# A mixture-of-experts decoder layer: TensorE's expert numbers read one a tile instead of sixteen at once

## The chip, the cores and the metric

The kernel runs on one core of a Trainium2 chip. The metric is the device time in microseconds (us) of one execution, the median of three. Besides the runs that only give a time there is one profiled execution, and every row below comes from it.

## The reference

One decoder layer on `x` of shape (8, 256, 256), with a context of (8, 120, 256). It has three parts, each followed by a layer norm: causal self-attention with 16 heads, a slot-attention block with a GRU cell in three iterations, and a feed-forward part with a shared MLP and 8 experts of which each token takes 2. The change touches the experts alone:

```python
router_probs = softmax(x @ gate_w + gate_b)
expert_values, expert_indices = top_k(router_probs, k=2)
expert_values = expert_values / (expert_values.sum(-1) + 1e-09)
h = gelu(einsum('bsd,edi->bsei', x, ew1) + eb1)        # D = 256, I = 1024, E = 8
all_outputs = einsum('bsei,eid->bsed', h, ew2) + eb2
moe_out = einsum('bse,bsed->bsd', weights_E, all_outputs)
return x + mlp(x, sh_w1, sh_b1, sh_w2, sh_b2) + moe_out
```

## The kernel before

All matmuls of the experts are done on two float16 halves of each number. The 2 x 2048 choices of the router are sorted by expert into tiles of 128 rows, each tile of one expert. There are `NTILE` = 39 tiles. Which expert a tile belongs to is known only at run time: VectorE writes the 39 numbers as integers into `tile_e`, one row of the on-chip memory, while the shared MLP still runs (line 2147).

The instructions of each engine are written out by hand and each engine takes its own in order, with semaphores between them. An engine that needs the expert of a tile reads it from `tile_e` into registers (`experts_from`, a TENSOR_LOAD), and every address of a weight is worked out from such a register. TensorE's program in the expert stage is a loop over `i`. In each round it turns the gathered rows of tile `i + 3` (`turn`, two transposes, line 1872), and then runs `tile_pair(i + 2, ..., i, ...)`: the first layer ("up") of tile `i + 2` mixed with the second layer ("down") of tile `i`. One `tile_pair` has eight chunks `k`. A chunk has six up matmuls of 128 columns (line 2254), one down matmul of 512 columns (line 2262) and one of 256 (line 2263). So a full round has 48 + 8 + 8 + 2 = 66 matmuls. The order of TensorE's program shows what stands between the matmuls for the addresses: in each chunk four instructions of line 2254 (the order calls them ISA, the trace FUSED_REGOPS) and one of line 2262 (REGISTER_ALU, in the trace ALU_OP). They compute with registers.

The expert numbers reach TensorE's registers in three reads, of at most `LOADED` = 16 numbers each. The first is in the shared MLP, two matmul groups before the first transposes (`first_experts`). The second stands in front of `tile_pair(16, ...)`, behind the transposes of tile 17. The third, of the last 7 numbers, stands in front of `tile_pair(32, ...)`:

```python
if (i + 2) % LOADED == 0:
    expert += experts_from(mybir.EngineType.PE, i + 2)
tile_pair(i + 2, expert[i + 2], i, expert[i])
```

VectorE (`experts_vector`) reads the same numbers for its own use in three such reads of its own. ScalarE does the gelu, VectorE the biases and the low halves, GpSimd gathers rows of later tiles and adds finished rows into memory by indirect DMA.
Of the kernel before, what the change touches and what calls it, by code (L numbers as in the profile page):

```python
# [34 lines left out]
def decoder_layer(nc, a, out):  # L35
# [5 lines left out]
    E, _, I = a["L0_ffn_ew1"].shape  # L41
# [11 lines left out]
    NTILE = 2 * T // P + E - 1  # L53
# [3 lines left out]
    with top:  # L57
        def sb(ctx, name, shape, dt=F32):
            return ctx.enter_context(nc.sbuf_tensor(name, shape, dt))
# [47 lines left out]
        tile_e = sb(top, "tile_e", [P, NTILE], I32)  # L107
# [368 lines left out]
        with ExitStack() as c:  # L476
# [90 lines left out]
            for j in range(LOW_FROM, ITEMS):  # L567
                for place, n in enumerate(room(j)):
                    n = min(n, LOW_SHARES * PIECES - made)
# [1109 lines left out]
        with ExitStack() as c:  # L1679
# [172 lines left out]
            LOADED = 16  # L1852
            first_experts = []

            def experts_from(engine, i):

                _, values = nc.values_load_multi_w_load_instructions(
                    tile_e[0:1, i:min(i + LOADED, NTILE)], engines=(engine,), min_val=0, max_val=E - 1,
                    skip_runtime_bounds_check_because="a count of at least zero, cut at E - 1 where it is made",
                    bass_reorder=False)  # L1860
                return list(values)

            def turn(i):

                PE.wait_ge(rows_in[i % 2], 16 * (i // 2 + 1))
                if i == 0:
                    PE.wait_ge(count_mm, 2)
                if i >= 1:
                    PE.wait_ge(g_lo, i)
                    PE.wait_ge(g_hi, i)  # L1870
                for ch in range(DC):
                    mm = PE.transpose(ps[:, 7, ch * P:ch * P + P], xg[:, i % 2, ch * P:ch * P + P], ident[:, :])  # L1872
                mm.then_inc(g_turned2, 1)
# [5 lines left out]
            def low_made(m):  # L1879

                return (H_low, m + 1) if m < MF else (H_late, m + 1 - MF)

            def up(m):
                g, k = m // IC, m % IC
                if m >= 2:
                    PE.wait_ge(H_gelu, m - 1)
                if m == 0:
                    PE.wait_ge(sw_in, 16 * SHARED_PIECES)
                    PE.wait_ge(tr_out, 2 * STEPS)
                if m == 1:  # L1890
                    PE.wait_ge(tz_out, 2 * STEPS)
                if m == MF:
                    PE.wait_ge(r_line, NAMED)
                if m == MF + 1:
                    PE.wait_ge(g_lo, NTILE)
                    PE.wait_ge(g_hi, NTILE)
                if k == 0:
                    PE.wait_ge(n_lo, g + 1)
                    PE.wait_ge(n_hi, g + 1)
                w = [[s1c[i][:, ch, k * P:k * P + P] for i in range(2)] for ch in range(DC)]  # L1900
                x = [[xT[:, g, i, ch, :] for i in range(2)] for ch in range(DC)]
                split_matmuls(PE, ps[:, late_bank(m), :], list(zip(w, x))).then_inc(H_mm, 1)

            def down_bank(g):
                return 4 if g == 1 else 2

            def down_tile(m, t):
                g, k = m // IC, m % IC
                w = [hh[m % 3][i][:, t * P:t * P + P] for i in range(2)]
                x = [s2c[i][:, k, :] for i in range(2)]  # L1910
                return split_matmuls(PE, ps[:, down_bank(g) + t // 2, t % 2 * D:t % 2 * D + D], [(w, x)],
                                     first=k == 0 and t % 2 == 0, last=k == IC - 1, skip_group_check=True)
# [334 lines left out]
            def experts_tensor():  # L2247
                def up_chunk(i, e, k):

                    u, q = i % 2, k // 4  # L2250
                    w = [[e1[:, bass.ds(e, 1), ch, h, k * P:k * P + P].squeeze(1) for h in range(2)]
                         for ch in range(DC)]
                    for n, (ch, (h, j)) in enumerate(itertools.product(range(DC), HILO)):
                        yield PE.matmul(ps[:, 2 * u + q, (k % 4) * P:(k % 4) * P + P], w[ch][h], xgT[u][j][:, ch, :],  # L2254
                                        start=n == 0, stop=n == 3 * DC - 1)

                def down_chunk(i, e, k):

                    u = i % 2  # L2260
                    w = e2[:, bass.ds(e, 1), k, :, :].squeeze(1).rearrange("p i n -> p (i n)")
                    yield PE.matmul(ps[:, 4 + u, :], he[u][0][:, k, :], w, start=k == 0, stop=False, skip_group_check=True)  # L2262
                    yield PE.matmul(ps[:, 4 + u, 0:D], he[u][1][:, k, :], w[:, 0:D], start=False, stop=k == IC - 1,  # L2263
                                    skip_group_check=True)

                def tile_pair(up, e_up, down, e_down):

                    if up is not None:
                        PE.wait_ge(g_lo, up + 1)
                        PE.wait_ge(g_hi, up + 1)  # L2270
                    if down is not None:
                        PE.wait_ge(U_lo, down + 1)
                        PE.wait_ge(U_hi, down + 1)
                        if down >= 2:
                            PE.wait_ge(D_out, 2 * (down - 1))
                    if up == 0:
                        PE.wait_ge(H_gelu, MF)
                    if up == 1:
                        PE.wait_ge(O_out, NG - 1)
                    if down == 0:  # L2280
                        PE.wait_ge(O_out, 2)
                    for k in range(IC):
                        if up is not None and up >= 2 and k % 4 == 0:
                            PE.wait_ge(U_bias, 2 * (up - 2) + k // 4 + 1)
                        ups = up_chunk(up, e_up, k) if up is not None else iter(())
                        downs = down_chunk(down, e_down, k) if down is not None else iter(())
                        for _ in range(2):
                            for mm in itertools.islice(ups, 3):
                                last_up = mm
                            for mm in itertools.islice(downs, 1):  # L2290
                                last_down = mm
                        if up is not None and k % 4 == 3:
                            last_up.then_inc(U_mm, 1)
                    if down is not None:
                        last_down.then_inc(D_mm, 1)

                def add_sums():

                    PE.wait_ge(made, 18)
                    for t in range(TG):  # L2300
                        if t % CT == 0:
                            PE.wait_ge(gathered[(EARLY + t) // CT], 16)
                        PE.matmul(ps[:, down_bank(NG - 1) + t // 2, t % 2 * D:t % 2 * D + D], ident_up, xs[:, EARLY + t, :],
                                  start=False, stop=False, skip_group_check=True)

                def last_downs():

                    for n in range(2):
                        for m in range(MS - 3, MS):  # L2310
                            if n == 0:
                                PE.wait_ge(*low_made(m))
                                PE.wait_ge(H_hi, m + 1)
                            for t in (2 * n, 2 * n + 1):
                                mm = down_tile(m, t)
                        mm.then_inc(O_mm, 1)

                PE.wait_ge(e_in, 16 * 2 * E)
                expert = first_experts
                tile_pair(0, expert[0], None, None)  # L2320
                turn(2)
                tile_pair(1, expert[1], None, None)
                for i in range(NTILE):
                    if i + 3 < NTILE:
                        turn(i + 3)
                    if i + 2 < NTILE:
                        if (i + 2) % LOADED == 0:
                            expert += experts_from(mybir.EngineType.PE, i + 2)
                        tile_pair(i + 2, expert[i + 2], i, expert[i])
                    else:  # L2330
                        up(MF + i - (NTILE - 2))
                        tile_pair(None, None, i, expert[i])
                for m in range(MF + 2, MS):
                    up(m)
                    if m - 2 < MS - 3:
                        down(m - 2)
                add_sums()
                last_downs()
# [234 lines left out]
```

## Time and profile before

| | before |
|---|---|
| time, median of 3 runs (lowest to highest) | 910.36 us (908.17 to 910.95) |
| the profiled execution: its own time | 910.25 us |
| its span, first to last instruction | 909.0 us |
| TensorE matmul busy in the span | 879.0 us (97%) |
| VectorE, ScalarE, GpSimd busy | 71%, 61%, 40% |
| mean granted TensorE clock | 0.998 |

The profiled execution's own time is 1.25 us longer than its span and lies within the runs. Busy shares are averages over stages; the stage of the change runs from 653 us to 880 us of the span.

### The profile page before, as it was taken

The numbers are of one execution on the slowest core, as the hardware profiler recorded it, in microseconds if no ns is written. First come the engines' busy times: TensorE is split into PE (matmuls) and PEld (weight loads), VectorE is DVE, ScalarE is ACT, GpSimd is POOL, SyncE is SP. The second block draws the span as 40 slices with busy tenths as digits, with TensorE's granted clock in tenths as the row PEclk, the third lists the DMA queues.
The fourth block names the chain that finished last, engine by engine and source line by source line (L and its number), as shares of the span: only waits on it lengthen the run. The fifth ranks groups of instructions, "written<-read, shape, count | busy, mean of one in ns | idle before, by whom it ended". The sixth has DMA issues, their size and how long they took to land. (4 is left out here: it accounts for less than half of the span.)

```text
span 909.0 us, 23841 instructions
## 1 busy us (share of the span) xinstructions
PE 879.0 (97%) x8190; PEld 670.8 (74%) x8190; DVE 649.0 (71%) x1839; ACT 557.5 (61%) x1347; POOL 365.4 (40%) x492
## 2 busy tenths in 40 slices
PE   5999999999999999999999999999999999999996
PEld 4777777777777777776666666666788888888864
DVE  4767688777676778667878787769677767776755
ACT  5777877777666677657575654645455545554555
POOL 2333434333323455325444442354534444444433
PEclk9999999999999999999999999999999999999999
DMA  9742434342323241230000000099443332333226
GB/s 320 193 140 94 147 107 153 106 140 94 133 75 123 96 158 49 9 93 1 1 1 2 1 1 2 17 361 409 134 113 50 49 49 44 49 49 48 42 29 191
DMA packets 61584, 88.09 MB, mean 97 GB/s; under 512 B 17279, under 2 KB 46527, under 8 KB 61343
## 3 DMA queue, kind: packets, MB, share of 16 engines
q1 hardware_dynamic: 53439, 75.52, 25.2%
q0 software_dynamic: 7488, 10.27, 7.1%
q8 instruction: 72, 1.18, 0.5%
q10 hardware_dynamic: 544, 0.79, 0.3%
q14 instruction: 41, 0.34, 0.1%
HBM read 56.00 MB, written 30.56 MB: 95 GB/s over the span
## 5 line engine op out<-in xcount | busy, mean ns | idle before, releaser
L2254 PE MATMUL ps<-slots,e 128*128 128x128 f16 x1872 | 189.9, 219 | 2.3 <-DVE xs L2421 2.2
L667 POOL TENSOR_SCALAR prob<-prob,rden 128x128 f32<-128x128 f32 (+1 forms) x256 | 110.6, 448 | 202.6 <-DVE rden L956 202.6
L2254 PEld LDWEIGHTS ps<-slots,e 128*128 x1872 | 152.4, 97 | 35.4 <-issue 5.0
L853 ACT ACTIVATE prob<-prob,nmx 128x128 f32<-128x128 f32 (+1 forms) x256 | 114.1, 450 | 41.6 <-DVE nmx L949 38.9
L2262 PE MATMUL ps<-e,xT 128*128 x312 | 117.3, 378 | 0.0
L2351 ACT ACTIVATE slots<-slots 128x512 f32<-128x512 f32 x78 | 49.0, 630 | 106.9 <-DVE slots L2405 103.1
L31 PE MATMUL ps<-xT,wqkv 128*128 128x256 f16 x768 | 97.2, 278 | 0.6 <-DVE wqkv L936 0.6
L31 PEld LDWEIGHTS ps<-xT,wqkv 128*128 128x128 f16 x768 | 70.9, 99 | 30.5 <-issue 22.2
L2263 PE MATMUL ps<-e,xT 128*128 x312 | 85.0, 273 | 0.0
L1766 POOL DMA_INDIRECT xg<-rows_x,dst x39 | 40.9, 1049 | 106.3 <-DVE mask L2394 103.2
L949 DVE CUSTOM_DVE_ANT_0 prob<-ps,mask 128x128 f32<-128x128 f32 (+1 forms) x256 | 75.9, 353 | 5.0 <-PE ps L747 5.0
L2410 DVE TENSOR_TENSOR xT<-slots,xT 128x1024 f16<-128x1024 f32 x39 | 47.8, 1225 | 40.0 <-ACT xT L2357 40.0
L2226 POOL DMA_INDIRECT back_y<-xs,dst x39 | 62.6, 1606 | 28.8 <-DMA back_y<-xs,dst 11.9
L2405 DVE SCALAR_TENSOR_TENSOR slots<-ps,b1e 128x512 f32<-128x512 f32 x78 | 53.5, 691 | 26.5 <-PE ps L2254 26.3
L963 DVE COPY pT<-ps 128x384 f32<-128x384 f32 x64 | 35.6, 556 | 40.8 <-PE ps L718 40.5
L747 PE MATMUL ps<-qk 64*128 64x128 f32 (+1 forms) x512 | 60.0, 353 | 0.8 <-ACT qk L863 0.7
L969 DVE TENSOR_TENSOR oT<-ps,oT 128x256 f16<-128x256 f32 x64 | 27.2, 424 | 46.5 <-ACT oT L877 46.0
L31 PE MATMUL ps<-an,wqkv 120*128 120x256 f16 x432 | 59.0, 272 | 1.0 <-POOL an L1500 1.0
L612 DVE SCALAR_TENSOR_TENSOR parted<-piece,parted 128x256 f16<-128x256 f32 x144 | 57.0, 420 | 0.0
L757 PE MATMUL ps<-pT,v 128*64 128x128 f32 x768 | 56.1, 281 | 0.7 <-DVE pT L963 0.7
L870 ACT COPY pT<-ps 128x384 f32<-128x384 f32 x64 | 30.6, 479 | 41.3 <-PE ps L718 40.0
L718 PE MATMUL ps<-ident,prob 128*128 128x128 f32 x384 | 52.7, 273 | 2.1 <-DVE oT L969 2.0
(275 smaller groups left out, 1940.5 us busy)
## 6 DMA issues: line engine op xcount, KB each, us to landing
halves<-parted SPq DMA_DIRECT2D x36, 512.0 KB, 2.9
piece<-in_L_ffn_ew SPq DMA_DIRECT2D x32, 512.0 KB, 4.4
e<-halves SPq DMA_DIRECT2D x16, 1024.0 KB, 15.4
piece<-in_L_ffn_sh_w SPq DMA_DIRECT2D x4, 512.0 KB, 8.8
sw<-halves SPq DMA_DIRECT2D x4, 512.0 KB, 6.7
rows_x<-xs SPq DMA_DIRECT2D x4, 512.0 KB, 7.1
xs<-back_y SPq DMA_DIRECT2D x8, 256.0 KB, 5.9
out<-xs SPq DMA_DIRECT2D x8, 256.0 KB, 2.1
```

Of the source, the lines that this page charges most:

```text
L31: mm = pe.matmul(out, w, x, start=first and n == 0, stop=last and n == len(products) - 1, **kw)
L612: VE.scalar_tensor_tensor(share(piece_part(q, 1)), share(like_part(q)), WS, share(piece_part(q, 0)), ALU.mult, ALU.subtract).then_inc(p_lo, 1)
L667: PO.tensor_scalar(prob[m % 3][:, h, r], prob[m % 3][:, h, r], rden[m % 2][:, h, t:t + 1], 1.0, ALU.mult, ALU.mult).then_inc(normed, 1)
L747: mm = PE.matmul(ps[:, 2 + h, query_tile(t)], qk[m % 2][r, 0, t * P:t * P + P], qk[m % 2][r, 1, 0:(t + 1) * P], start=True, stop=True)
L757: mm = PE.matmul(ps[r, 4 + t, 384:512], v_sb[m // 2 % 2][:, key, m % 2, r], pT[:, h, at:at + P], start=key == 0, stop=key == t, skip_group ...
L853: SC.activation(p, p, ACT.Exp, bias=nmx[u][:, h, t:t + 1], scale=-1.0, accum_out=den[u][:, h, t:t + 1]).then_inc(exped, 1)
L949: VE.tensor_tensor_reduce(prob[m % 3][:, h, r], ps[:, 2 + h, r], mask[:, r], -1.0, HIGHEST, ALU.add, ALU.min, nmx[m % 2][:, h, t:t + 1]).t ...
L2226: PO.indirect_dma_start(back_y, bass.IndirectOffsetOnAxis(ap=dst[:, i:i + 1], axis=0), yo[i % 2], None, compute_op=ALU.add).then_inc(rows_ ...
L2254: yield PE.matmul(ps[:, 2 * u + q, (k % 4) * P:(k % 4) * P + P], w[ch][h], xgT[u][j][:, ch, :], start=n == 0, stop=n == 3 * DC - 1)
L2262: yield PE.matmul(ps[:, 4 + u, :], he[u][0][:, k, :], w, start=k == 0, stop=False, skip_group_check=True)
L2263: yield PE.matmul(ps[:, 4 + u, 0:D], he[u][1][:, k, :], w[:, 0:D], start=False, stop=k == IC - 1, skip_group_check=True)
L2405: VE.scalar_tensor_tensor(z, ps[:, 2 * u + q, :].rearrange("p (k t) -> p k t", k=4), 1 / WS, bias, ALU.mult, ALU.add).then_inc(U_bias, 1)
```

## The change

TensorE's reads in front of `tile_pair(16)` and `tile_pair(32)` go. In their place `tile_pair` itself, after its second chunk (`k == 1`), reads one number, that of the next tile. It does so from `up` = 15 on to `up` = 37, so for the tiles 16 to 38, which makes 23 reads. The read in the shared MLP stays, with the numbers of tiles 0 to 15, and VectorE's reads stay as they are.

```diff
-            def experts_from(engine, i):
+            def experts_from(engine, i, n=LOADED):
 
                 _, values = nc.values_load_multi_w_load_instructions(
-                    tile_e[0:1, i:min(i + LOADED, NTILE)], engines=(engine,), min_val=0, max_val=E - 1,
+                    tile_e[0:1, i:min(i + n, NTILE)], engines=(engine,), min_val=0, max_val=E - 1,
@@ tile_pair
                         if up is not None and k % 4 == 3:
                             last_up.then_inc(U_mm, 1)
+                        if up is not None and k == 1 and LOADED <= up + 1 < NTILE:
+                            expert.extend(experts_from(mybir.EngineType.PE, up + 1, 1))
@@ the loop of experts_tensor
                     if i + 2 < NTILE:
-                        if (i + 2) % LOADED == 0:
-                            expert += experts_from(mybir.EngineType.PE, i + 2)
                         tile_pair(i + 2, expert[i + 2], i, expert[i])
```

On TensorE of the kernel before, at the boundary to `tile_pair(16)`, the read stands behind the two transposes of tile 17 and ahead of the register work and the first matmuls of the new tile (`e` stands for the weights, `slots` and `xT` for the activations, `ps` for the accumulators):

```order
L2254 MATMUL ps<-slots,e 128x128
L2263 MATMUL ps<-e,xT 128x256
L1872 MATMUL ps<-ident,xg 128x128 [waits g_hi,g_lo,rows_in1]
L1872 MATMUL ps<-ident,xg 128x128
L1857 TENSOR_LOAD tile_e
L2254 ISA [waits U_hi,D_out,U_lo,U_bias,g_hi,g_lo]
L2254 MATMUL ps<-slots,e 128x128 x2
L2254 ISA
L2254 MATMUL ps<-slots,e 128x128
```

In the changed kernel nothing stands at that boundary; the transposes are followed directly by the register work of the new tile.

On TensorE of the changed kernel, inside `tile_pair(15)`, where the number of tile 16 is read, behind the last matmul of chunk 1 and ahead of the register work of chunk 2:

```order
L2262 MATMUL ps<-e,xT 128x512
L2254 ISA
L2254 MATMUL ps<-slots,e 128x128 x2
L2254 ISA
L2254 MATMUL ps<-slots,e 128x128
L2263 MATMUL ps<-e,xT 128x256
L1857 TENSOR_LOAD tile_e
L2254 ISA
L2254 MATMUL ps<-slots,e 128x128 x2
```

The same place recurs in each of the 23 rounds up to `tile_pair(37)`. TensorE's program has 24 TENSOR_LOAD in place of 3, and no other instruction is added, taken away or reordered. The programs of the other engines are the same as before.

## Rows read from the trace of the kernel before

**Rows 1.** The page: span, busy time by engine, granted clock, start of the chain.

```profile
span 909.0 us, 23841 instructions
...
PE 879.0 (97%) x8190; PEld 670.8 (74%) x8190; DVE 649.0 (71%) x1839; ACT 557.5 (61%) x1347; POOL 365.4 (40%) x492
...
PEclk9999999999999999999999999999999999999999
...
PE ps L2254 12%; PE ps L2262 7%; PE ps L31 5%; PE ps L2263 4%; DMA back_y<-xs,dst 1%; PE ps L1872 1%; DMA xs<-back_y 1%; DMA xg<-rows_x,dst 0%; DVE routes L2491 0%; PE ps L1133 0%; POOL slots L1836 0%; SPq L2460 0%; ACT slots L1984 0%; DVE xs L2513 0%; PE ps L1095 0%
```

**Rows 2.** Stages: length; busy (count) of PE, PEld, DVE, ACT, POOL; clock; DMA share, GB/s.

```profile
661.16:740.26 79.10, 79.06 (x927) 66.90 (x926) 55.71 (x112) 41.74 (x70) 34.26 (x27) 1.00 0.31 59
740.26:747.16 6.90, 5.79 (x69) 4.75 (x68) 4.04 (x8) 3.21 (x6) 3.24 (x4) 1.00 0.27 44
747.16:826.33 79.17, 79.16 (x927) 66.96 (x926) 55.21 (x112) 41.52 (x70) 35.32 (x28) 1.00 0.30 48
...
831.97:838.82 6.85, 5.72 (x68) 4.71 (x67) 4.04 (x8) 3.21 (x6) 3.23 (x4) 1.00 0.28 45
838.82:861.42 22.60, 22.60 (x268) 19.14 (x266) 15.71 (x32) 11.67 (x20) 9.19 (x8) 1.00 0.30 47
```

**Rows 3.** Line 1857, the reads: duration in ns, first and last start.

```profile
L1857 DVEq TENSOR_LOAD <-tile_e x3: 1249/1289/1349, 643.6 to 834.6; - x3
L1857 PEldq TENSOR_LOAD <-tile_e x3: 1077/1125/1291, 645.0 to 831.9; - x3
```

**Rows 4.** Timeline, 740 to 742 us: start, length, work, idle before and releaser.

```profile
740.26 0.38 PE L1872 MATMUL ps<-ident,xg 128*128 128x128 f32 x2
...
741.74 0.29 PEld L2254 LDWEIGHTS ps<-slots,e 128*128 x3 [1.34 <-issue]
741.75 0.42 PE L2254 MATMUL ps<-slots,e 128*128 128x128 f16 x3 [1.11 <-DVE xs L2421]
```

**Rows 5.** Lines 1857 and 2273 (the next wait) ahead of tile pairs 16, 18, 32.

```profile
L1857 PEldq TENSOR_LOAD <-tile_e x1: 1125/1125/1125, 740.1 to 740.1; - x1
L2273 PEldq EVENT_SEMAPHORE  x1: 51/51/51, 741.3 to 741.3; - x1
L2273 PEldq EVENT_SEMAPHORE  x1: 51/51/51, 752.7 to 752.7; - x1
L1857 PEldq TENSOR_LOAD <-tile_e x1: 1077/1077/1077, 831.9 to 831.9; - x1
```

**Rows 6.** Line 1870, the wait before the transposes of tile 19, ahead of tile pair 18.

```profile
L1870 PEldq EVENT_SEMAPHORE  x1: 51/51/51, 752.5 to 752.5; - x1
```

**Rows 7.** The read in the shared MLP, and the next wait behind it.

```profile
L1857 PEldq TENSOR_LOAD <-tile_e x1: 1291/1291/1291, 645.0 to 645.0; - x1
L1917 PEldq EVENT_SEMAPHORE  x1: 51/51/51, 646.4 to 646.4; - x1
```

**Rows 8.** Timeline of TensorE, 645 to 662 us.

```profile
645.00 1.46 PE L31 MATMUL ps<-xT,sw 128*128 128x512 f16 x6
...
646.30 1.47 PE L31 MATMUL ps<-sw,slots 128*128 128x256 f16 x12
647.61 1.46 PE L31 MATMUL ps<-xT,sw 128*128 128x512 f16 x6
...
653.28 2.98 PE L2254 MATMUL ps<-slots,e 128*128 128x128 f16 x48
656.77 0.44 PE L1872 MATMUL ps<-ident,xg 128*128 128x128 f32 x2 [0.51 <-DMA xg<-rows_x,dst]
657.05 4.19 PE L2254 MATMUL ps<-slots,e 128*128 128x128 f16 x48
661.16 0.41 PE L1872 MATMUL ps<-ident,xg 128*128 128x128 f32 x2
```

**Rows 9.** Line 2254, 748.60 to 748.65 us: the register work before chunk 2 of tile pair 17.

```profile
L2254 PEldq FUSED_REGOPS  x1: 46/46/46, 748.6 to 748.6; - x1
```

**Rows 10.** Timeline of TensorE around it.

```profile
748.57 0.33 PE L2254 MATMUL ps<-slots,e 128*128 128x128 f16 x3
748.73 0.27 PE L2263 MATMUL ps<-e,xT 128*128 x1
748.84 0.33 PE L2254 MATMUL ps<-slots,e 128*128 128x128 f16 x3
```

## The prediction

> **What bounds the kernel now.** I read the page first. TensorE's matmuls are busy for 97% of the span, no other engine for more than 71%, and the chain that ended last runs through TensorE's expert lines 2254, 2262 and 2263 [rows 1]. So the stage is paced by TensorE, and time added to or taken from its rounds shows in the total. "TensorE" here can be two things: the array, or the sequencer that feeds it. A read of registers is the sequencer's work, so I have to know which of the two paces a round.
>
> For that I cut the stage at the transposes that open each round [rows 2]. 14 rounds without a read took 79.10 us, another 14 took 79.17, and 4 took 22.60, which is 5.65 us a round each time. What would the array alone need? Three matmuls of 128 columns follow each other in 0.16 us [rows 10], so 0.055 each; 6 of 512 columns take 1.30 us and 12 of 256 take 1.31 [rows 8], so 0.217 and 0.109. A round is 48 x 0.055 + 8 x 0.217 + 8 x 0.109 + 2 x 0.109 for the transposes = 5.47 us. The array is 0.18 us short of the measured round. The sequencer is the other candidate. The first layer of tile 1 runs without down matmuls, and its 48 matmuls took from 657.05 to 661.16 us, 4.11 us or 86 ns each instead of 55 [rows 8]. Nothing but the 32 register instructions of line 2254 stands between them, so those take about 0.128 us each on the sequencer, and in a full round 8 more of line 2262 and the waits of the boundary are added. That comes to about the 5.65 us of the round. The sequencer is therefore as much the bound as the array, and cannot build up a store of matmuls. Rows 9 and 10 show how little it has: the register instruction ahead of chunk 2 starts between 748.60 and 748.65, the chunk's first matmul at 748.84. It is 0.2 us ahead.
>
> **What the change removes.** Two reads at a boundary. The rounds that hold them took 6.90 and 6.85 us where 5.65 is usual [rows 2], so they cost 1.25 and 1.20 us, together 2.45. The timeline shows the first as an idle array between the transposes and 741.75 [rows 4]. The row names a VectorE instruction as the releaser. I don't follow that: the weight load beside it is put down to "issue", that is, to no other engine, and the read itself explains it. It starts at 740.1 and lasts 1.125 us, and the next wait on the sequencer is at 741.3 [rows 5]. Ahead of tile pair 18, without a read, the same two waits stand at 752.5 and 752.7 [rows 5, 6]. So the sequencer does nothing else while a read is under way, and the cost was visible in full although the array still had the transposes to do.
>
> **What it adds.** 23 reads of one number. The trace has no read of one number. It has 16 numbers in 1.125 us and 7 in 1.077 [rows 5], which is 5 ns a number, so nearly all of a read is a fixed time and one number should take 1.125 - 15 x 0.0053 = 1.045 us. VectorE's three reads, 1.249 to 1.349 us, say the same of the fixed part [rows 3]. What came on top of the read's own duration was 1.25 - 1.125 = 0.125 and 1.20 - 1.077 = 0.123 us. I take 1.045 + 0.124 = 1.17 us for each new read.
>
> **What covers them.** In the middle of a tile there are matmuls before and after the read, but the array can only work on what the sequencer has already handed over, and that is 0.2 us of work. So I expect the array to stand idle for 0.9 to 1.0 us behind each read. The 0.2 us is no lasting gain either: at the boundary of each round the sequencer has four waits to pass and the array runs dry there anyhow, so a sequencer that is 1.17 us late arrives 1.17 us late. The rounds of tiles 16 and 32 paid in full in the same way, with a read that began before the last transposes did.
>
> **What is queued behind a read**: the matmuls of chunks 2 to 7 of the same tile pair. VectorE (line 2405) waits for the up half of them, ScalarE for VectorE, GpSimd's add for the down half. All of these get late with TensorE and by the same amount, and they are less busy than it, so they add nothing. No wait and no DMA is moved past another.
>
> **The sum.** 23 x 1.17 = 26.9, less 2.45, gives 24.5 us more. On the profiled execution's 910.25 us that is **934.7 us**; this execution lies 0.1 us from the median, 910.36. Bounds of the unknown price: at the low end the read's 1.045 us less all of the 0.24 us lead, 0.80 us each, which gives 23 x 0.80 - 2.45 = +16.0 and 926.2 us. At the high end the longest read of TensorE, 1.291 us [rows 7], and 0.124, so 1.415 each: +30.1 and 940.4 us. I stay near the two rows of this stage, because the new reads fall into it, with a DMA share near 0.3 as there [rows 2].
>
> The Trainium skill, in "Runtime: NRT & Kernel Launch", section "The ~15µs preamble/postamble breakdown", puts a TENSOR_LOAD at about 1.3 us, one trip to HBM for a few words. Taken as the price of old and new reads alike, with the same 0.124 us, this would be 21 x 1.42 = +29.9 us. The rows here are shorter, and the sum goes by them.
>
> **Rival 1: the reads are hidden, and the time falls or stays.** If matmuls enough were queued, a read in the midst of them would cost nothing, and only the 2.45 us of the two old ones would go: 910.25 - 2.45 = 907.8 us. For it speaks the read in the shared MLP. The sequencer began it at 645.0 us [rows 7], while its place in the program is behind the 12 matmuls that started at 646.30, and groups follow each other at 645.00, 646.30 and 647.61 without a gap [rows 8]. There 18 matmuls, 2.6 us of work, were handed over ahead, and a read of 1.291 us vanished. It is decided by the lead: from 1.17 us on it is hidden. There, no register instruction stands among the matmuls; here the lead is 0.2 us [rows 9, 10]. I give it 6 in 100.
>
> By the Trainium skill, "TensorE: Matmul & The Clock Gate", section "Architectural detail: the array is 16× 32×32, not 1× 128×128", TensorE's queue holds 64 instructions. A full queue would be 32 matmuls with their weight loads, an estimate of 32 / 66 of a round or 2.7 us, and by that rule this rival would win. The trace shows a queue that deep could not be filled in this stage.
>
> **Rival 2: the reads are hidden in part.** The array's own work is 0.18 us short of a round, and a lead that one place in one tile shows as 0.2 us may be larger at others. If both shortened the gap for good, each read would cost the low bound or somewhat less: 920 to 929 us, most likely 926. Against it: rounds 16 and 32 show no saving. 10 in 100.
>
> **Rival 3: reads of one number are longer than I take them**, as the one in the shared MLP was with 1.291 us: 938 to 942 us. It began with a gather under way; gathers and adds run through this stage as well, but neither of its two reads was above 1.125. 8 in 100.
>
> **Rival 4: the clock.** Each round of the changed kernel will have an idle gap of about 1 us. Rounds 16 and 32 had one, with the matmuls busy for 5.79 of 6.90 us, and the granted clock stayed at 1.00 (2.4 GHz) there [rows 2]. A row with many such rounds on end does not exist. If the clock fell to 1.2 GHz the array's 5.47 us would double, 5.47 x 23 = 126 us over the 23 rounds and far outside my range. 1 in 100.
>
> **How the numbers follow.** 75 in 100 go to the forecast, with its own range 930 to 938 us. With rival 2's most likely time and most of rival 3 the range is 926 to 940. A measurement of this kernel tells about 0.3%, 2.7 us, from no change. Only rival 1 comes near that: its 907.8 us is 0.27% below, so its 6 in 100 are split between faster and same. All others are slower.
>
> **What the profile of the changed kernel would show.** Line 1857 on PEldq x24, with a median near 1.05 us; rounds between transposes of 5.65 us up to tile pair 14, 6.8 us from 15 to 37, with 16 and 32 now like their neighbours; a gap of 0.9 to 1.0 us in the array in each of these rounds, in front of the first matmul of chunk 2; matmul busy time unchanged. I am wrong if these gaps are absent or below 0.7 us, if the reads are above 1.2 us, or if the granted clock leaves 1.00.

## The result, and the profile after

| | before | after |
|---|---|---|
| median | 910.06 us (908.17 to 911.94, 6 runs) | 913.78 us (913.57 to 916.24, 6 runs) |
| the profiled execution's own time; its span | 910.25; 909.0 us | 914.44; 913.2 us |

The ratio is 1.005 with a 95% interval of 1.004 to 1.0059, while the two medians alone lie 3.7 us apart: the kernel is slower by some 4 to 5 us, where I had forecast 24.5 and a range from 926 us up. The direction was right, the size wrong by a factor of about five.

The page of the changed kernel, beside [rows 1]:

```profile
span 913.2 us, 23862 instructions
PE 882.9 (97%) x8190; PEld 671.1 (73%) x8190; DVE 649.4 (71%) x1839; ACT 557.2 (61%) x1347; POOL 365.4 (40%) x492
```

The stage cut at the transposes, beside [rows 2] (length, busy time and count of PE, PEld, DVE, ACT, POOL, clock, DMA share, GB/s). The first row holds the 13 rounds ahead of the first new read, the second the 22 rounds up to the last transposes; the 23rd read is behind them:

```profile
659.42:732.90 73.48, 73.44 (x860) 62.12 (x859) 51.84 (x104) 38.68 (x65) 31.70 (x25) 1.00 0.32 62
732.90:864.83 131.93, 130.06 (x1455) 106.34 (x1453) 87.07 (x176) 65.93 (x111) 56.82 (x45) 1.00 0.29 46
```

73.48 / 13 = 5.65 us for a round without a read, as before. 131.93 / 22 = 6.00 us with one. So a read costs 0.34 us here, not 1.17. The row of line 1857, beside [rows 3], says why:

```profile
L1857 PEldq TENSOR_LOAD <-tile_e x24: 297/301/1307, 643.4 to 866.2; - x24
```

24 reads as foreseen, but the median is 0.301 us. The timeline of TensorE at one of them, which lasted 0.301 us from 752.4 on (columns: start, length, work):

```profile
752.53 0.27 PE L2263 MATMUL ps<-e,xT 128*128 x1
752.85 0.35 PE L2254 MATMUL ps<-slots,e 128*128 128x128 f16 x3
```

and among the weight loads:

```profile
752.84 0.22 PEld L2254 LDWEIGHTS ps<-slots,e 128*128 x3 [0.27 <-issue]
```

The next matmul would be due 0.11 us after 752.53, at 752.64; it starts at 752.85. The view reports no idle time here, since the modelled end of the matmul before (752.80) reaches nearly to it; among the weight loads it stands as 0.27 us, put down to issue. That is also why matmul busy time rose, by 5.5 us in this stage and by 3.9 us in all, with the same 8190 matmuls, where I had foretold no change. A gap of 0.2 us has to be read from starts, not from busy time.

The sum with the measured price is 23 x 0.34 - 2.45 = +5.4 us. The two profiled executions differ by 4.2. The stage from the transposes of tile 3 to those of tile 38 took 205.41 us for 200.26 (+5.2), what follows 48.37 for 47.58 (+0.8, of which the 23rd read is 0.34), and what comes ahead of it, where the programs are the same, 1.7 us less. That last part is no effect of the change; the last section has where it comes from.

### The profile page after: what moved, and what is told of

Read it like the earlier page. It is cut to its first block and busy times, and to the rows that moved or that the text cites. A ratio compares the mean times of both kernels' runs of the same rounds, so it can differ in the third digit from the quotient of the medians.

```text
span 913.2 us, 23862 instructions
## 1 busy us (share of the span) xinstructions
PE 882.9 (97%) x8190; PEld 671.1 (73%) x8190; DVE 649.4 (71%) x1839; ACT 557.2 (61%) x1347; POOL 365.4 (40%) x492
```

## The experiments

Theory A: the number of values sets the length of a read. Theory B: the place does, since the reads of before stood behind transposes and the new ones amid matmuls. A third, theory C, came out of the experiment with other sizes. Apart from what sets the read's length there is the question whether the sequencer's small lead is what lets a read be seen.

### One a tile at the boundary

```diff
-                        if (i + 2) % LOADED == 0:
-                            expert += experts_from(mybir.EngineType.PE, i + 2)
+                        if i + 2 >= LOADED:
+                            expert += experts_from(mybir.EngineType.PE, i + 2, 1)
```

> One number a tile as in the changed kernel, but read at the tile boundary, behind the transposes, where the kernel before has its two reads. Theory A (the number of values decides how long a read takes): 23 reads of 0.30 us, rounds of 6.0 us, the time of the changed kernel within 1 us, so 913 to 915 us. Theory B (the place decides: short amid matmuls, long behind the transposes): 23 reads of about 1.05 us, rounds of 6.8 us, 933 to 936 us.

Measured: 917.13 us, ratio to before 1.0088 (1.0069 to 1.0107). Line 1857, and the 21 rounds from the transposes of tile 17 to those of tile 38:

```profile
L1857 PEldq TENSOR_LOAD <-tile_e x24: 298/303/1305, 645.1 to 872.8; - x24
```

```profile
740.13:867.05 126.92, 121.34 (x1388) 100.97 (x1387) 83.12 (x168) 62.90 (x106) 54.67 (x43) 1.00 0.29 46
```

Reads of 0.30 us, rounds of 126.92 / 21 = 6.04 us. Theory B falls: behind the transposes a read of one is as short as amid matmuls. The cost of 0.39 us is 0.05 more than inside the tile, which over 23 reads is 1.2 us. The time lay above the 913 to 915 us that theory A gave. The two profiled executions, 2.7 us apart, say where that comes from: this one reached the transposes of tile 3 at 661.05 us and that of the changed kernel at 659.42, with the same program up to there (see "Two beginnings" below), and the remaining 1.1 us is what the reads cost more here. One read, the last, took 0.508 us, and no run shows why.

### Sixteen inside the tile

```diff
+                        if up is not None and k == 1 and (up + 1) % LOADED == 0 and up + 1 < NTILE:
+                            expert.extend(experts_from(mybir.EngineType.PE, up + 1))
@@ the reads ahead of tile_pair(16) and tile_pair(32) go
```

> Sixteen and seven numbers at once as before, but read behind chunk 1 of tile pairs 15 and 31, where the changed kernel reads. Theory A: two reads of 1.13 and 1.08 us, two rounds of 6.85 us instead of 5.65, the time of the kernel before within 1 us. Theory B: two reads of 0.30 to 0.40 us, two rounds of 6.0 us, about 1.7 us faster than before.

Measured: 909.22 us, ratio 1.0001 (0.999 to 1.0012). All three reads:

```profile
L1857 PEldq TENSOR_LOAD <-tile_e x3: 1085/1123/1295, 643.5 to 826.2; - x3
```

The two late reads took 1.123 and 1.085 us, their rounds 6.81 and 6.77 us. Theory A holds again: the place does not change the read's length. The rounds are 0.09 us shorter each than the 6.90 and 6.85 of before, too little to show in the time.

### Other sizes

```diff
-                        if up is not None and k == 1 and LOADED <= up + 1 < NTILE:
-                            expert.extend(experts_from(mybir.EngineType.PE, up + 1, 1))
+                        if up is not None and k == 1 and up + 1 in READS:
+                            expert.extend(experts_from(mybir.EngineType.PE, up + 1, READS[up + 1]))
# first kernel: READS = {16: 1, 17: 2, 19: 3, 22: 4, 26: 5, 31: 8}; second: READS = {16: 6, 22: 7, 29: 10}
```

`READS` gives for each read the tile number with which it begins and how many numbers it takes.

> The 23 numbers of tiles 16 to 38 in reads of 1, 2, 3, 4, 5 and 8, each behind chunk 1 of a tile pair. Theory A with a step: reads up to some size take 0.30 us each, those above 1.05 us or more, and nothing lies between. Theory A with a slope: 0.30, 0.43, 0.56, 0.69, 0.82 and 1.08 us. Theory B: all of them 0.30 to 0.35 us. In each case a round with a read is longer than 5.65 us by the read's duration and 0.04 to 0.12 us.

> The same with reads of 6, 7 and 10 numbers. Theory A with a step: 0.30 us up to the step and 1.05 to 1.10 us above it. With a slope: 0.95, 1.08 and 1.09 us. Theory B: all 0.30 to 0.35 us.

Measured: 912.71 and 913.6 us in one run each. The reads in their order, of the first kernel:

```profile
L1858 PEldq TENSOR_LOAD <-tile_e x1: 324/324/324, 734.7 to 734.7; - x1
L1858 PEldq TENSOR_LOAD <-tile_e x1: 553/553/553, 740.8 to 740.8; - x1
L1858 PEldq TENSOR_LOAD <-tile_e x1: 779/779/779, 752.6 to 752.6; - x1
L1858 PEldq TENSOR_LOAD <-tile_e x1: 1007/1007/1007, 770.4 to 770.4; - x1
L1858 PEldq TENSOR_LOAD <-tile_e x1: 1372/1372/1372, 794.1 to 794.1; - x1
L1858 PEldq TENSOR_LOAD <-tile_e x1: 2230/2230/2230, 823.7 to 823.7; - x1
```

and of the second:

```profile
L1858 PEldq TENSOR_LOAD <-tile_e x1: 841/841/841, 736.1 to 736.1; - x1
L1858 PEldq TENSOR_LOAD <-tile_e x1: 1971/1971/1971, 770.9 to 770.9; - x1
L1858 PEldq TENSOR_LOAD <-tile_e x1: 2587/2587/2587, 812.5 to 812.5; - x1
```

None of the three forms that I had written down fits. Reads of 1, 2, 3, 4, 5, 7, 8 and 10 numbers grow by some 0.25 us a number, with hardly a fixed part and no end at 1.1 us. But six numbers took 0.84 us, less than four; seven took 1.97, while before the last seven took 1.077 and sixteen 1.125 [rows 5]. The short ones begin at place 16 or 32 of the row, the long ones at 17, 19, 22, 26, 29 or 31. This is theory C: four numbers go in one piece if their place is divisible by four, all others singly, and a piece takes about 0.27 us. Sixteen at 16 are 4 pieces (1.125), seven at 32 are 1 + 3 (1.077), six at 16 are 1 + 2 (0.841), ten at 29 are 10 (2.587). The fours are counted from the read's own first number: the eight at 31 and the ten at 29 contain the numbers 32 to 35, whose place would do, and yet they took 2.230 and 2.587 us, the time of eight and of ten pieces, where five and seven would be about 1.4 and 1.9. So a read that begins off a multiple of four goes number by number throughout.

### Fours, aligned and shifted

`READS = {16: 4, 20: 4, 24: 4, 28: 4, 32: 4, 36: 3}` in the one kernel, `{16: 1, 17: 4, 21: 4, 25: 4, 29: 4, 33: 4, 37: 2}` in the other.

> The numbers of tiles 16 to 38 in reads of four that begin at 16, 20, 24, 28 and 32, and one of three at 36, each behind chunk 1 of a tile pair. Theory C (a read goes in pieces, each of about 0.27 us; four numbers are one piece if the first has a place divisible by four, all others are a piece each): the reads of four take 0.30 us, the one of three 0.8 us; rounds 5.98 us five times and 6.5 once; together 2.5 us over rounds without a read, so the time of the kernel before within 1 us. Rival D (the number of values alone decides, 0.25 us each): reads of 1.0 us, six rounds of 6.6 to 6.7 us, 6 us in all, 3.5 us slower than before.

> The same with the reads of four shifted by one, at 17, 21, 25, 29 and 33, one number at 16 and two at 37. Theory C: 1.0 to 1.1 us for each read of four, as for the one of four at 22 in the kernel with reads of 1, 2, 3, 4, 5 and 8, 0.30 and 0.55 us for the others; rounds of 6.7 us; 5.9 us in all over rounds without a read, 3 to 4 us slower than before. Rival D: the same 1.0 us, so only the comparison with the aligned reads tells them apart.

Measured: 910.18 us, ratio 1.0008 (0.9999 to 1.0018), and 914.12 us in one run. All reads of the aligned kernel, and the last of it (of three numbers):

```profile
L1858 PEldq TENSOR_LOAD <-tile_e x7: 332/345/1292, 643.5 to 849.3; - x7
L1858 PEldq TENSOR_LOAD <-tile_e x1: 778/778/778, 849.3 to 849.3; - x1
```

One of the shifted reads of four:

```profile
L1858 PEldq TENSOR_LOAD <-tile_e x1: 1007/1007/1007, 789.9 to 789.9; - x1
```

The other shifted ones took 1.242, 1.017, 0.998 and 1.000 us. The rounds with a read of four were 6.03 to 6.06 us in the aligned kernel and 6.65 to 7.00 in the shifted one. Same number of values, three times the duration: theory C, and rival D falls.

### The same places, another address

```diff
-        tile_e = sb(top, "tile_e", [P, NTILE], I32)
+        tile_e = sb(top, "tile_e", [P, NTILE + 1], I32)[:, 1:NTILE + 1]
```

> The aligned reads of four of two runs ago (at 16, 20, 24, 28, 32 and three at 36), but the row of numbers begins one number later in memory. If the address decides what goes as one piece, each read of four takes 1.0 us as in the kernel with shifted places, the first read of sixteen more than the 1.3 us of before, about 4 us, and the rounds with a read of four 6.7 us. If the place in the row decides, nothing changes: 0.34 us and rounds of 6.03 us.

Measured: 915.05 us in one run. All reads of TensorE, those of VectorE, and the timeline of TensorE around its first:

```profile
L1858 PEldq TENSOR_LOAD <-tile_e x7: 763/1009/3992, 643.7 to 855.9; - x7
```

```profile
L1858 DVEq TENSOR_LOAD <-tile_e x3: 1622/3618/3852, 642.3 to 840.1; - x3
```

```profile
644.99 1.47 PE L31 MATMUL ps<-sw,slots 128*128 128x256 f16 x12
647.77 1.46 PE L31 MATMUL ps<-xT,sw 128*128 128x512 f16 x6 [1.30 <-issue]
```

The places are those of the aligned kernel, and yet the reads of four take 1.01 us, and the sixteen early ones 3.99, which is sixteen pieces. So it is the address. The early read now shows, too: 3.99 us less the 2.6 us that the sequencer is ahead there leaves 1.3 us of idle array.

VectorE's reads became long in the same way, and one of them cost time on TensorE. It began at 743.99 us and lasted 3.618. Behind it stands VectorE's work on the turned rows, for which TensorE waits before the next transposes (line 1871 here, a wait of 1.53 us from 746.67 on). That round took 6.94 us with no read of TensorE in it:

```profile
741.31:748.25 6.94, 5.86 (x69) 4.74 (x67) 3.17 (x6) 2.35 (x4) 1.01 (x1) 1.00 0.21 32
```

So a longer read on an engine that does not set the pace can cost time too, when others wait for what stands behind it. The 915.05 us therefore hold more than TensorE's own reads.

### Fixed addresses

```diff
                     u, q = i % 2, k // 4
+                    if k:
+                        e = i % E
@@ and the same in down_chunk
```

> The changed kernel, but only chunk 0 of each tile takes its weights by the register; the other seven chunks use a fixed expert, so 1404 of 1560 register instructions are gone (weights of other experts are used, the work of the array is the same). If the sequencer paces the stage and its small lead is why a read is seen, the rounds fall to the array's own 5.5 us with and without a read, and the 23 reads cost nothing: below 903 us in all. Rival: a read stops the array itself; then rounds with a read stay 0.3 us longer than rounds without.

Measured: 901.62 us in one run. Ten rounds ahead of the first late read, and 21 with a read in each:

```profile
677.57:732.55 54.98, 54.98 (x662) 44.67 (x661) 39.51 (x80) 29.87 (x51) 25.76 (x21) 1.00 0.30 50
738.05:853.52 115.47, 115.47 (x1390) 93.70 (x1388) 83.16 (x168) 62.74 (x106) 53.38 (x43) 1.00 0.30 50
```

54.98 / 10 and 115.47 / 21 are both 5.50 us. With the register work gone the rounds fall from 5.65 us to about the 5.47 that I had worked out for the array, and 23 reads of 0.302 us in the median vanish completely. The rival, a read that stops the array itself, falls. The read of 754.57 us shows the lead: the chunk behind it started on the array at 756.09, so the sequencer was 1.5 us ahead, where in the kernel before it is about 0.1 us ahead at the first chunk of a round and 0.3 at the last. What makes a read visible is that the sequencer has almost no lead.

### Thirty-two early, eight late

The row gets a fortieth number, a copy of the last, so that the last read is two full pieces. A small copy on VectorE is added for it, and VectorE's own third read has eight numbers too.

```diff
                         first_experts.extend(experts_from(mybir.EngineType.PE, 0))
+                        first_experts.extend(experts_from(mybir.EngineType.PE, LOADED))
# READS = {32: 8}; tile_e is NTILE + 1 long
```

> The numbers of tiles 0 to 15 and 16 to 31 in two reads in the shared MLP, and those of tiles 32 to 38 and a fortieth that is not used in one read of eight behind chunk 1 of tile pair 31. Theory C: the early reads, 1.1 to 1.3 us each, are hidden by the 2.6 us that the sequencer is ahead there; the late one is two pieces, 0.55 us, and its round 6.25 us; 0.6 us in place of the 2.45 of before, so 1.8 us faster, ratio 0.998. If the two early reads are seen, their 2.5 us less the lead come on top, and it is no faster than before.

Measured: 907.3 us, ratio 0.9973 (0.9961 to 0.9985). The late read, the reads of VectorE, and the round of the late one, behind 28 rounds and ahead of 5:

```profile
L1858 PEldq TENSOR_LOAD <-tile_e x1: 602/602/602, 826.4 to 826.4; - x1
```

```profile
L1858 DVEq TENSOR_LOAD <-tile_e x3: 595/1248/1350, 643.7 to 833.9; - x3
```

```profile
666.90:824.95 158.05, 158.05 (x1852) 133.79 (x1850) 111.16 (x225) 83.95 (x141) 71.26 (x56) 1.00 0.29 48
824.95:831.26 6.31, 5.93 (x69) 4.92 (x68) 3.95 (x8) 3.24 (x6) 2.97 (x4) 1.00 0.27 44
831.26:859.55 28.29, 28.29 (x332) 23.86 (x331) 19.75 (x40) 14.74 (x25) 12.34 (x10) 1.00 0.30 49
```

The two early reads, 1.288 and 1.112 us, leave no gap: the matmul groups around them start at 645.03, 646.33, 647.64 and 648.93 us as in [rows 8]; the round of the late one costs 6.31 - 5.65 = 0.66 us. VectorE's read of eight took 0.595 us, half of what its read of seven took before (1.249): one number more made two full pieces of four pieces. This version is faster than both, by 0.3% than the kernel before. That all 39 are read early was not tried.

## Why the prediction was wrong

**The step that failed** is the price of a new read, "one number should take 1.125 - 15 x 0.0053 = 1.045 us". I drew a line through two reads, of 16 and 7 numbers, and took what it gave at nought as a fixed time. In truth both were four pieces, and so were VectorE's three, which I called on for the fixed part. None of them shows what one piece takes, and a read of one piece is 0.30 us. With it and the 0.04 us that came on top, the sum is +5.4 us instead of +24.5; this step is 17 us of the 19 that I was off. The low bound of 0.80 us had the same flaw: it took off the lead, but left the read at 1.045. For a kind of read that the trace does not have, the floor should have been close to nothing. A warning stood in the rows: more than twice the values for 0.05 us more looks like a fixed time, but two reads with the same number of steps look just the same.

**The time on top** was 0.125 and 0.123 us in the rounds of before and 0.04 us inside the tile, 0.09 at the boundary in the run with one a tile there. This second term was mis-sized by some 0.08 us a read, 1.9 us in all.

**What held**: that the sequencer does nothing else during a read; that its lead of 0.2 us does not cover it; that what it loses is not made up, since rounds with a read in the tile are longer by about the read's own duration, whatever the size (0.30: 6.00 us; 1.12: 6.81; 2.23: 7.87 in the kernel with a read of eight); that the two reads removed were worth 2.45 us; that the clock stays at 1.00 with one gap a round. Rounds 16 and 32 are now like their neighbours, and the busy time of the other engines moved by less than 0.5 us. The fixed addresses show that the sequencer, and not the array, makes the round 5.65 us instead of 5.50. My own sign of being wrong, gaps below 0.7 us, is what came: they are about 0.2.

**The rivals.** Hidden reads (rival 1) did not come, but under fixed addresses they do, and there the sequencer gets far enough ahead, as in the shared MLP. The result lies between the 907.8 us of rival 1 and the 920 us of rival 2, and rival 2's reason, a gap made smaller by the lead, is not what the trace shows. Rivals 3 and 4 did not come, though one longer gap in another kernel was followed by the fall of the clock that rival 4 speaks of (below).

**The 1.3 us of the Trainium skill** for a TENSOR_LOAD, taken in the prediction from "Runtime: NRT & Kernel Launch", section "The ~15µs preamble/postamble breakdown", is given there for registers loaded from HBM, while `tile_e` lies on the chip. Of TensorE's reads here those of four pieces, 1.00 to 1.31 us, and the one of five, 1.37, come near it; a read of one is 0.30 us and one of sixteen single pieces 3.99 us.

## What to carry to other kernels

Before costing a read of values into registers, look where it begins. If its first number lies at an aligned place, count its groups of four and each number left over; if not, count every number. Rounding a read up to a full group can make it shorter, as eight numbers were against seven. Whether a read is seen at all depends on the sequencer's lead: in a place where the sequencer is further ahead than the read is long, as in the matmul groups without register work here, it costs nothing. Where a new size of an instruction has to be priced from two old ones, ask whether the two may be the same number of steps, and let the range go down to one step.

## What the runs showed of the hardware

**Pieces by address.** A TENSOR_LOAD of TensorE took 0.30 to 0.35 us for one number or an aligned four, with one exception of 0.51, and 1.0 us (once 1.24) for a four that begins one number off. The same four moved by one number in memory, at the same place of the row, went from 0.34 to 1.01 us.

**The clock fell once behind a long gap.** In the kernel with reads of 6, 7 and 10, the read of ten left the array idle, and behind it the granted clock was one half for 3.4 us. The timeline row, then the round around it, the seven rounds behind it, and the stretch at half clock:

```profile
815.29 0.35 PE L2255 MATMUL ps<-slots,e 128*128 128x128 f16 x3 [2.36 <-issue]
```

```profile
811.02:820.98 9.96, 7.60 (x69) 5.75 (x67) 3.98 (x8) 3.24 (x6) 4.35 (x4) 0.83 0.35 54
820.98:859.47 38.49, 38.49 (x464) 31.52 (x463) 27.74 (x56) 20.55 (x35) 16.13 (x13) 1.00 0.27 43
816.65:820.07 3.42, 3.42 (x24) 2.45 (x22) 0.69 (x1) 0.63 (x1) 1.76 (x2) 0.50 0.40 63
```

The round took 9.96 us, 4.3 more than usual, for a read of 2.59; 3.4 us at half speed are worth the other 1.7. Granted 0.50 is 1.2 GHz. While the array ran at that level the sequencer got ahead: its lead rose from 0.27 us at 816.4 to 1.84 at 818.5, and it was back at 0.13 by 859.6. In between seven rounds took 38.49 / 7 = 5.50 us each, the array's own time. So part of the loss came back at 0.15 us a round. The fall was seen once; behind a read of 2.23 us in the other kernel, with 1.97 us of idle array and a round of 7.87, the clock stayed at 1.00. That the gap caused the fall was not tested.

**Two beginnings.** The profiled executions reach the transposes of tile 3 at one of two times, about 659.4 or 661.1 us, although up to there the programs of before, after and most of the others are the same. The two kernels compared here lie on different sides. The first matmuls of line 747 of before, and then of after:

```profile
13.99 1.65 PE L747 MATMUL ps<-qk 64*128 64x128 f32 x8 [0.75 <-ACT qk L863]
```

```profile
13.90 0.93 PE L747 MATMUL ps<-qk 64*128 64x128 f32 x8 [0.75 <-ACT qk L863]
```

The same eight matmuls took 1.65 us in the one and 0.93 in the other, and the twelve of line 31 behind them 2.51 and 1.48. TensorE came to its full rate later in the former and lost 1.7 us by it. The traces' record of the granted clock fits this: it begins, at 1.00, at 17.7 us in the kernel before and at 13.4 in the changed one, and in all eleven traces at 12.9 to 13.8 or at 17.7 to 18.7 us; the views take the clock as 1.00 ahead of it too. The six traces in which it begins early are those that reach tile 3 early (the one with the row moved in memory does so but for its 1.3 us of idle array). The times look the same: the sixteen runs of the kernel before beside the aligned fours lie at 908.2 to 908.3 or 909.5 to 910.3 us, with none between. What sets the one or the other beginning is not shown. The 1.7 us is a third of the effect that was to be measured here, and it is why rounds, counted within one execution, tell more than the difference of two spans.
